# Adaptive layer norm, attention and mixture of experts on one core: layer-norm rows with a scalar-tensor-tensor, the input split on GpSimd, and two transposes ahead of the projection

## The chip, the cores and the metric

One core of one Trainium2 chip runs the whole program. The metric is the device time of one execution in microseconds (us); the number compared is the median of the runs. The engines are TensorE (PE, matmuls, with its weight loads PEld), VectorE (DVE), ScalarE (ACT), GpSimd (POOL) and SyncE (SP, which only issues DMAs here).

## The reference, cut to what matters

Eight batch items of 512 tokens with 128 channels go through an attention with 16 heads of 64, with normalised queries and keys, and then through a mixture of eight experts with a shared branch. The change touches the first part:

```python
h = _layernorm(x, axis=-1) * (1 + ca) + sa
x = x + ga * _L0_attn_ref(h, Wq, Wk, Wv, Wo, bo, q_scale, k_scale)
h = _layernorm(x, axis=-1) * (1 + cb) + sb
# in _L0_attn_ref, for each batch item b and head:
q = _l2norm(h @ Wq.T) * q_scale ; k = _l2norm(h @ Wk.T) * k_scale ; v = h @ Wv.T
attn = softmax(q @ k.T * DH ** -0.5) ; out = (attn @ v) @ Wo.T + bo
```

## The kernel before, in words

**Units and slots.** Work is cut into 64 units u = 8 b + hp: batch item b, head pair hp (two heads, 0 to 7). The attention loop has one slot for each unit, and a slot has four places, called `pair` in the code and counted from 0 to 3; place p handles the 128 query rows of tile p for both heads. Batch item 0 and the last one are written out, items 1 to 6 run in a hardware loop. Each engine has its own instruction stream in an order fixed by hand, and runs it in that order; semaphores are the only tie between engines. There is no scheduler.

**TensorE in one place of slot u.** `project` (L486 to L488) makes queries, keys and values of unit u+2 for one token tile, three matmuls in a split precision (a rounded high part and a low part); at place 0 one step of the residual stream follows (`between`: a part of the output projection L567 to L569, or a transpose of layer-norm rows L585, of y L577, or the router L593); at place 1 `inverse_rows` (L543) transposes the inverse row sums of unit u-1; at place 2 `transpose_q` (L495) transposes the normalised queries of unit u+1, at place 3 `transpose_k` (L502) its keys; then come `scores` (L516), `transpose_probs` (L532) and `weigh_values` (L556). All three transposes write one PSUM bank, XT_BANK, which is also the bank of `between`.

**The other engines in a slot.** ACT copies the projection out of PSUM (L676), copies the inverse rows (L707) and the high part of queries (L685) and keys (L690), and computes exponentials (L697). DVE takes the row maxima (L815), two at each place, the low parts of queries (L803) and keys (L810), the sum of squares of the next unit (L792) and at the slot's start the inverse of the row sums (L826). POOL starts its slot with `widen` (L993, waits for L826), then `normalise_qk`: twelve small Newton steps (L49 to L55) and two multiplications (L987), the first for queries and the second for keys, each with its own count of `qn_done`; then one square (L977), `split_o` (L999, L1001), and three more squares. `transpose_q` waits for the first L987.

**Layer norm.** In slots 0 and 3 of a batch item `norm_first` puts `ln_rows` (L200, four instructions of 128x128) at place 3 in front of the row maxima on DVE, and the TensorE transposes of those rows (L585) stand at place 0 of slots 1 and 4. These wait for `kl_done` as well, which L810 of place 3 sets after the row maxima. In slots 0 and 3 POOL also runs `inverse_std`, twelve more small steps, before its squares.

**The input split.** `split_h1` (L844, L846) turns the modulated input h1_out of the next batch item into a high part hT_h and a low part hT_l, one 128-token tile at a time. It runs on DVE, at places 1, 2 and 3 of slot 5 and place 0 of slot 6. Projections of the next item start in slot 6, place 0, and wait there for `hT_ready`. For item 0 the four tiles are split before the loop.

Of the kernel before, what the change touches and what calls it, by code (L numbers as in the profile page):

```python
# [5 lines left out]
P = 128  # L6
ALU = mybir.AluOpType
# [53 lines left out]
def adaln_attention_moe(nc, x, Wq, Wk, Wv, Wo, bo, q_scale, k_scale, proj_w, proj_b, expert_bias,  # L61
# [16 lines left out]
    with ExitStack() as whole:  # L78
# [62 lines left out]
        with ExitStack() as scope:  # L141
# [25 lines left out]
            def tile_of(b, t):  # L167

                return x1_all[:, bass.ds(b * NT + t, 1)].rearrange("p o c -> p (o c)")
# [26 lines left out]
            def ln_rows(dve, b, count):  # L196
                dve.wait_ge(ln_step, NEWTON_OPS * (count + 1))
                after(dve, hlnT_ready, count)
                for t in range(NT):
                    last = nc.vector.tensor_scalar(h_ln[:, t], tile_of(b, t), mean_var[:, t, 0:1], rstd[:, t:t + 1],  # L200
                                                   ALU.subtract, ALU.mult)
                last.then_inc(hln_done, 1)


# [258 lines left out]
            with nc.Block() as block:  # L463
# [13 lines left out]
                def _(pe):  # L477
# [144 lines left out]
                    def slot(b, hp, main=True):  # L622

                        u = HP * b + hp
                        earlier = units_before(b, hp)
                        side = (kl_done, u + 1 if main else u)
                        for pair in range(NT):
                            if main and with_next(b, hp, 2):
                                project(u + 2, hp + 2, b + (hp + 2) // HP, pair)
                            if main and pair == 0:  # L630
                                side = between(b, hp, u)
                            if pair == 1 and earlier >= 1:
                                inverse_rows(u - 1, side)
                                side = (r_copied, u)
                            if main and pair == 2 and with_next(b, hp, 1):
                                transpose_q(u + 1, hp + 1, side)
                            if main and pair == 3 and with_next(b, hp, 1):
                                transpose_k(u + 1, hp + 1)
                            if main:
                                scores(u, hp, pair)  # L640
                            if pair < 2 and earlier >= 1:
                                transpose_probs(u - 1, pair + 2)
                            if pair >= 2 and main:
                                transpose_probs(u, pair - 2)
                            if pair < 2 and earlier >= 2:
                                weigh_values(u - 2, hp - 2, pair + 2)
                            if pair >= 2 and earlier >= 1:
                                weigh_values(u - 1, hp - 1, pair - 2)
# [23 lines left out]
                def _(act):  # L672
# [59 lines left out]
                    def slot(b, hp, main=True):  # L732
                        u = HP * b + hp
                        earlier = units_before(b, hp)
                        for pair in range(NT):
                            if main and with_next(b, hp, 2):
                                copy_projection(u + 2, hp + 2, pair)
                            if pair == 0 and main:
                                if hp == Y_HP[0]:
                                    gate_y(b)  # L740
                                if hp == H1T_HP and not is_const(b, LAST):
                                    modulate1(b + 1)
                                if hp == H2T_HP and not is_const(b, 0):
                                    modulate2(b - 1)
                            if pair == 1 and earlier >= 1:
                                copy_inverse(u - 1, hp - 1)
                            if main and pair == 2 and with_next(b, hp, 1):
                                high_q(u + 1, hp + 1)
                            if main and pair == 3 and with_next(b, hp, 1):
                                high_k(u + 1, hp + 1)  # L750
                            if main:
                                exponentials(u, hp, 2 * pair)
                                exponentials(u, hp, 2 * pair + 1)
                            if pair == 1 and earlier >= 1:
                                copy_transposed(u - 1, hp - 1, 3)
                            if pair == 3 and main:
                                copy_transposed(u, hp, 1)
                            if main and pair == 1 and hp == H2T_HP and not is_const(b, 0):
                                keep_h2(b - 1)
# [27 lines left out]
                def _(dve):  # L787
# [49 lines left out]
                            last = nc.vector.tensor_copy(dst[:, k:k + 1], modT[:, v, bass.ts(b, 1)])  # L837
                        last.then_inc(done, 1)

                    def split_h1(b, t):  # L840
                        dve.wait_ge(h1_done, b + 1)
                        after(dve, pj_ready, NT * (HP * b - 1) + t + 1)
                        toks = slice(t * P, (t + 1) * P)
                        nc.vector.tensor_copy(hT_h[:, toks], h1_out[:, toks]).then_inc(h1h_done, 1)  # L844
                        dve.wait_ge(h1h_done, NT * b + t + 1)
                        nc.vector.tensor_tensor(hT_l[:, toks], h1_out[:, toks], hT_h[:, toks].bitcast(F32),  # L846
                                                ALU.subtract).then_inc(hT_ready, 1)

                    def add_y(b, k):
                        dve.wait_ge(y_ready, NT * b + k + 1)  # L850
                        if k == 1:
# [39 lines left out]
                    def norm_first(b, hp, pair):  # L891

                        rows = norm_of(b, hp)
                        if rows and pair == 1:
                            stats_there(dve, rows[1])
                        if rows and pair == 3:
                            ln_rows(dve, *rows)
                        if not is_const(b, LAST) and (hp, pair) in ((5, 1), (5, 2), (5, 3), (6, 0)):
                            split_h1(b + 1, (pair - 1) % NT)

                    def norm_last(b, hp, pair):

# [41 lines left out]
                            slot(b, hp)  # L944

                    take_mod(mod1, (CA, SA), 0, mod1_done, (h1_done, 0))
                    for t in range(NT):
                        split_h1(0, t)
                    sum_squares(0)
                    guess_norms(0)  # L950
                    low_q(0, 0)
# [19 lines left out]
                def _(pool):  # L971
# [17 lines left out]
                    def widen(u, hp):  # L989
# [4 lines left out]
                                                c1.unsqueeze(2).unsqueeze(3).to_broadcast([P, NT, 2, DH]),  # L994
                                                ALU.mult).then_inc(wide_done, 1)

                    def split_o(u, hp):
                        pool.wait_ge(o_done, u + 1)
                        nc.gpsimd.tensor_tensor(oT_h[:, hp % HP], oT[:], c1.to_broadcast([P, N]), ALU.mult).then_inc(oh_done, 1)  # L999
# [4 lines left out]
                    def slot(b, hp, main=True):  # L1004
# [14 lines left out]
                        if main and with_next(b, hp, 2):  # L1019
                            for t in range(1, NT):  # L1020
                                square_projection(u + 2, hp + 2, t)

                    def batch(b):
                        for hp in range(HP):
                            slot(b, hp)

                    normalise_qk(0, 0)
                    for t in range(NT):
                        square_projection(1, 1, t)
# [626 lines left out]
```

## Time and profile before

| | |
|---|---|
| median of 3 runs | 1407.26 us (1405.85 to 1416.08) |
| profiled execution, its own time | 1406.78 us |
| span of its instructions | 1405.0 us |
| mean granted TensorE clock | 0.959 of full speed |
| PE busy / DVE busy / ACT busy / POOL busy | 1262.1 / 1107.3 / 952.9 / 858.0 us |

The attention loop takes the stretch from about 43 to 1060 us, the routing and the experts the rest. In the timelines a row of several instructions (x4) gives the first start and the time from there to the last end. A bracket at a row's end gives the idle time of the engine in front of it and who ended it.

### The profile page before, as it was taken

What the parts mean: (1) busy time and instruction counts of PE and PEld (TensorE: products, weight loads), DVE (VectorE), ACT (ScalarE), POOL (GpSimd) and SP (SyncE); (2) the same over time, 40 slices, a digit from 0 to 9 for tenths busy, and PEclk for the clock granted to TensorE, in tenths of its full rate; (3) what the DMA queues carried; (4) which work ended last, traced back from release to release, by engine and by line L of the source; (5) the groups of instructions that cost most, each with busy time, mean ns of one, the idle gap of its engine ahead of it and who ended that gap; (6) DMA issues with size and microseconds to landing.
All of it is one profiled execution on the core that took longest, in us unless ns stands there. A gap on an engine that the chain in (4) does not pass through costs nothing. (4 is left out here: it accounts for less than half of the span.)

```text
span 1405.0 us, 31811 instructions
## 1 busy us (share of the span) xinstructions
PE 1262.1 (90%) x9674; PEld 828.6 (59%) x9674; DVE 1107.3 (79%) x1995; ACT 952.9 (68%) x2014; POOL 858.0 (61%) x1659
## 2 busy tenths in 40 slices
PE   4899999989999999999899999999994477899997
PEld 4555565656555565556566555666552355677775
DVE  3778878878878887788788788877873996788887
ACT  3677677767666776677677766777762565777776
POOL 2577666766666776666667667676754664444443
PEclk8899999999999999999999999999998699999999
DMA  5000000000000000000000000000002000535341
GB/s 131 2 2 1 2 1 2 2 4 2 1 4 2 2 2 4 2 2 2 4 1 2 3 2 2 2 1 2 2 1 75 1 0 9 131 86 104 89 89 38
DMA packets 53202, 28.60 MB, mean 20 GB/s; under 512 B 8720, under 2 KB 51224, under 8 KB 53016
## 3 DMA queue, kind: packets, MB, share of 16 engines
q1 hardware_dynamic: 51832, 25.99, 7.7%
q8 instruction: 84, 1.38, 0.4%
q14 instruction: 102, 0.84, 0.2%
q10 hardware_dynamic: 1184, 0.40, 0.1%
HBM read 24.16 MB, written 2.23 MB: 19 GB/s over the span
## 5 line engine op out<-in xcount | busy, mean ns | idle before, releaser
L697 ACT ACTIVATE probs<-bank,neg_max 128x512 f32<-128x512 f32 x512 | 347.5, 684 | 280.3 <-DVE neg_max L815 259.5
L815 DVE TENSOR_REDUCE neg_max<-bank 128x1 f32<-128x512 f32 x512 | 329.3, 685 | 165.4 <-PE bank L516 162.0
L556 PE MATMUL bank<-probsT,qkv 128*64 128x512 f32 x1024 | 280.7, 628 | 0.9 <-DVE oT L832 0.9
L516 PE MATMUL bank<-operands 64*128 64x512 f32 x1536 | 255.9, 439 | 0.9 <-DVE operands L810 0.5
L993 POOL TENSOR_TENSOR inv_wide<-inv_sum,consts 128x512 f32<-128x512 f32 x64 | 66.5, 1039 | 237.7 <-DVE inv_sum L826 237.7
L532 PEld LDWEIGHTS T<-ident,probs 64*128 64x128 f32 x4096 | 173.6, 142 | 40.3 <-issue 10.2
L532 PE MATMUL T<-ident,probs 64*128 64x64 f32 x4096 | 173.6, 226 | 1.5 <-issue 0.7
L486 PEld LDWEIGHTS bank<-operands,hT_h 128*128 128x128 f32 x254 | 48.2, 190 | 213.0 <-issue 209.4
L516 PEld LDWEIGHTS bank<-operands 64*128 64x128 f32 x1536 | 128.4, 190 | 63.5 <-issue 44.2
L1627 POOL TENSOR_TENSOR hid_l<-gated,hid_h 128x512 fp32r<-128x512 f32 x64 | 89.4, 1397 | 123.3 <-ACT hid_h L1544 123.3
L977 POOL TENSOR_TENSOR sq<-qkv 128x256 f32<-128x256 f32 x252 | 150.9, 615 | 11.9 <-ACT qkv L676 9.7
L821 DVE COPY probsT<-T 128x1024 f32<-128x1024 f32 x128 | 155.5, 1215 | 0.1
L1605 DVE TENSOR_TENSOR gated<-probsT,act_out 128x512 f32<-128x512 f32 x128 | 125.5, 990 | 36.5 <-ACT act_out L1558 24.2
L676 ACT ACTIVATE qkv<-bank 128x384 f32<-128x384 f32 x254 | 125.1, 493 | 21.5 <-PE bank L488 18.2
L987 POOL TENSOR_TENSOR qkv<-qkv,rn 128x512 f32<-128x512 f32 x128 | 131.5, 1048 | 5.0
L702 ACT ACTIVATE probsT<-T 128x1024 f32<-128x1024 f32 x128 | 130.8, 1022 | 0.1
L486 PE MATMUL bank<-operands,hT_h 128*128 128x384 f32 x254 | 113.1, 445 | 10.9 <-issue 9.4
L697 ACT ACTIVATION_READ_ACCUMULATOR probs<-bank,neg_max 128x1 f32 x512 | 100.8, 197 | 0.0
L1544 ACT ACTIVATE hid_h<-gated 128x512 fp32r<-128x512 f32 x128 | 80.3, 627 | 27.5 <-DVE gated L1605 26.9
L488 PE MATMUL bank<-operands,hT_l 128*128 128x384 f32 x254 | 86.9, 342 | 0.0
L487 PE MATMUL bank<-wqkv_l,hT_h 128*128 128x384 f32 x254 | 86.5, 341 | 0.0
L792 DVE TENSOR_REDUCE ss<-sq 128x16 f32<-128x1024 f32 x64 | 77.3, 1208 | 10.9 <-issue 7.1
(235 smaller groups left out, 2399.7 us busy)
## 6 DMA issues: line engine op xcount, KB each, us to landing
probsT<-gate_scratch SPq DMA_DIRECT2D x64, 256.0 KB, 4.9
out<-x_all SPq DMA_DIRECT2D x8, 256.0 KB, 2.3
probsT<-in_L_ffn_fc_w SPq DMA_DIRECT2D x1, 1024.0 KB, 9.4
raw<-in_L_attn_Wq SPq DMA_DIRECT2D x1, 512.0 KB, 4.4
raw<-in_L_attn_Wk SPq DMA_DIRECT2D x1, 512.0 KB, 7.3
raw<-in_L_attn_Wv SPq DMA_DIRECT2D x1, 512.0 KB, 8.6
raw_o<-in_L_attn_Wo SPq DMA_DIRECT2D x1, 512.0 KB, 8.7
probsT<-in_L_ffn_sh_w SPq DMA_DIRECT2D x2, 256.0 KB, 2.7
```

The source lines that it names most:

```text
L486: nc.tensor.matmul(o, hT_h[:, toks], wqkv_h[:, :, cols], start=True, stop=False)
L516: last = nc.tensor.matmul(s_bank(hp, 2 * pair + head)[:], own[rows, q, toks], own[rows, k], start=((q, k) == (QH, KH)), stop=(q == QL))
L532: last = nc.tensor.transpose(T2[:, half, at:at + DH], probs[rows, (2 * pair + head) % 4, j * P:(j + 1) * P], ident[rows, rows])
L556: last = nc.tensor.matmul(O_BANK[rows, :], qkv[:, hp % 4, j, cols], probsT[:, hp % 2, head, j], start=(j == 0), stop=(j == NT - 1), skip_g ...
L676: nc.scalar.activation(qkv[:, hp % 4, t], bank[:, 0:3 * P], ACT.Copy).then_inc(pj_copied, 1)
L697: nc.scalar.activation(probs[:, i % 4], s_bank(hp, i)[:], ACT.Exp, bias=neg_max[:, i:i + 1], accum_out=row_sum[:, hp % 2, i:i + 1]).then_i ...
L702: nc.scalar.activation(pair_tiles(hp, pair), t_pair, ACT.Copy).then_inc(t_act, 1)
L815: nc.vector.reduce_max(neg_max[:, i:i + 1], s_bank(hp, i)[:], AX.X, negate=True).then_inc(max_done, 1)
L821: nc.vector.tensor_copy(pair_tiles(hp, pair), t_pair).then_inc(t_dve, 1)
L977: nc.gpsimd.tensor_tensor(sq[:, t], qk, qk, ALU.mult).then_inc(sq_done, 1)
L987: nc.gpsimd.tensor_tensor(rows, rows, by, ALU.mult).then_inc(qn_done, 1)
L1605: nc.vector.tensor_tensor(gated[:, k % 4], gate_rows[:, k // 2], act_out[:, k % 4], ALU.mult).then_inc(gated_done, 1)
```

## The change

Three edits. First, `ln_rows` uses `scalar_tensor_tensor` in place of `tensor_scalar`: the mean is still a scalar per partition, but the inverse deviation is now a second tensor input in SBUF, broadcast along the row. Second, `split_h1` moves from DVE to POOL: the copy that rounded the high part becomes a multiplication by a column of ones, and all four tiles stand at the end of POOL's slot 5 (HP - 3), after the last square. For item 0 they stand in front of POOL's first `normalise_qk`. Third, in every slot `inverse_rows` at place 1 and `transpose_q` at place 2 stand in front of `project` on TensorE, and `copy_inverse` and `high_q` stand in front of `copy_projection` on ACT. The step `between` still follows the projection of place 0, and `transpose_k` that of place 3.

```diff
                 for t in range(NT):
-                    last = nc.vector.tensor_scalar(h_ln[:, t], tile_of(b, t), mean_var[:, t, 0:1], rstd[:, t:t + 1],
-                                                   ALU.subtract, ALU.mult)
+                    last = nc.vector.scalar_tensor_tensor(out=h_ln[:, t], in0=tile_of(b, t), scalar=mean_var[:, t, 0:1],
+                                                          in1=rstd[:, t:t + 1].to_broadcast([P, C]), op0=ALU.subtract,
+                                                          op1=ALU.mult)
...
                         for pair in range(NT):
-                            if main and with_next(b, hp, 2):
-                                project(u + 2, hp + 2, b + (hp + 2) // HP, pair)
-                            if main and pair == 0:
-                                side = between(b, hp, u)
                             if pair == 1 and earlier >= 1:
                                 inverse_rows(u - 1, side)
                                 side = (r_copied, u)
                             if main and pair == 2 and with_next(b, hp, 1):
                                 transpose_q(u + 1, hp + 1, side)
+                            if main and with_next(b, hp, 2):
+                                project(u + 2, hp + 2, b + (hp + 2) // HP, pair)
+                            if main and pair == 0:
+                                side = between(b, hp, u)
...
                         for pair in range(NT):
+                            if pair == 1 and earlier >= 1:
+                                copy_inverse(u - 1, hp - 1)
+                            if main and pair == 2 and with_next(b, hp, 1):
+                                high_q(u + 1, hp + 1)
                             if main and with_next(b, hp, 2):
                                 copy_projection(u + 2, hp + 2, pair)
...
-                        if not is_const(b, LAST) and (hp, pair) in ((5, 1), (5, 2), (5, 3), (6, 0)):
-                            split_h1(b + 1, (pair - 1) % NT)
...
+                    def split_h1(b, t):
+                        pool.wait_ge(h1_done, b + 1)
+                        after(pool, pj_ready, NT * (HP * b - 1) + t + 1)
+                        toks = slice(t * P, (t + 1) * P)
+                        nc.gpsimd.tensor_tensor(hT_h[:, toks], h1_out[:, toks], c1.to_broadcast([P, P]), ALU.mult).then_inc(h1h_done, 1)
+                        pool.wait_ge(h1h_done, NT * b + t + 1)
+                        nc.gpsimd.tensor_tensor(hT_l[:, toks], h1_out[:, toks], hT_h[:, toks].bitcast(F32),
+                                                ALU.subtract).then_inc(hT_ready, 1)
...
+                        if main and hp == HP - 3 and not is_const(b, LAST):
+                            for t in range(NT):
+                                split_h1(b + 1, t)
```

TensorE at place 2 of slot 2 of item 0, before. L486 to L488 are the projection, L495 the transposes of the queries, L516 the scores, L556 the weighted values of place 1, and a bracket names the semaphores waited for:

```order
L556 MATMUL bank<-probsT,qkv 64x512 x2
L486 MATMUL bank<-operands,hT_h 128x384 [waits pj_copied]
L487 MATMUL bank<-wqkv_l,hT_h 128x384
L488 MATMUL bank<-operands,hT_l 128x384
L495 MATMUL bank<-ident,qkv 128x128 [waits r_copied,qn_done]
L495 MATMUL bank<-ident,qkv 128x128 x3
L516 MATMUL bank<-operands 128x512 [waits p_done]
L516 MATMUL bank<-operands 128x512 x5
```

The same place after the change; each line number is one higher:

```order
L557 MATMUL bank<-probsT,qkv 64x512 x2
L496 MATMUL bank<-ident,qkv 128x128 [waits r_copied,qn_done]
L496 MATMUL bank<-ident,qkv 128x128 x3
L487 MATMUL bank<-operands,hT_h 128x384 [waits pj_copied]
L488 MATMUL bank<-wqkv_l,hT_h 128x384
L489 MATMUL bank<-operands,hT_l 128x384
L517 MATMUL bank<-operands 128x512 [waits p_done]
L517 MATMUL bank<-operands 128x512 x5
```

The transposes and their waits now stand directly behind the weighted values of the place before, and the projection stands between them and the scores. At place 1 the transposes of `inverse_rows` move in the same way.

POOL at the end of slot 5 and the start of slot 6 of item 0, before; L977 is the square, L993 `widen`:

```order
L999 TENSOR_TENSOR oT_h<-oT,consts 128x512 [waits o_done]
L1001 TENSOR_TENSOR oT_l<-oT,oT_h 128x512 [waits oh_done]
L977 TENSOR_TENSOR sq<-qkv 128x256 [waits pj_copied] x3
L993 TENSOR_TENSOR inv_wide<-inv_sum,consts 128x512 [waits r_ready,inv_done]
L49 TENSOR_TENSOR rn_t<-rn 128x16 [waits rn_guess]
L51 TENSOR_TENSOR rn_t<-rn_t,ss_half 128x16 [waits rn_step]
```

The same place after the change; L965 is the square, L989 and L991 are the split, L981 is `widen`, and the line of dots stands for three more pairs of L989 and L991:

```order
L998 TENSOR_TENSOR oT_l<-oT,oT_h 128x512 [waits oh_done]
L965 TENSOR_TENSOR sq<-qkv 128x256 [waits pj_copied] x3
L989 TENSOR_TENSOR hT_h<-h_out,consts 128x128 [waits pj_ready,h1_done]
L991 TENSOR_TENSOR hT_l<-h_out,hT_h 128x128 [waits h1h_done]
...
L981 TENSOR_TENSOR inv_wide<-inv_sum,consts 128x512 [waits r_ready,inv_done]
L49 TENSOR_TENSOR rn_t<-rn 128x16 [waits rn_guess]
```

The eight instructions of the split stand in front of `widen` of slot 6 and of the Newton steps behind it.

## Rows read from the trace of the kernel before

**Rows 1.** the page's first part: busy time of each engine

```profile
PE 1262.1 (90%) x9674; PEld 828.6 (59%) x9674; DVE 1107.3 (79%) x1995; ACT 952.9 (68%) x2014; POOL 858.0 (61%) x1659
```

**Rows 2.** who waited for whom: us in total, times, longest us

```profile
POOL inv_wide L993 <- DVE inv_sum L826: 237.7, 63, 5.7
...
PE bank L585 <- DVE operands L810: 33.2, 14, 2.7
...
PE bank L495 <- POOL qkv L987: 9.0, 10, 5.6
```

**Rows 3.** timeline of DVE, slot 3, place 3, item 4; start us, us taken, engine

```profile
609.67 3.40 DVE L200 TENSOR_SCALAR h_ln<-x_all,mean_var,rstd 128x128 f32 x4
```

**Rows 4.** timeline of POOL in the same stretch

```profile
610.02 1.04 POOL L999 TENSOR_TENSOR oT_h<-oT,consts 128x512 fp32r<-128x512 f32 x1
611.14 1.28 POOL L1001 TENSOR_TENSOR oT_l<-oT,oT_h 128x512 fp32r<-128x512 f32 x1
612.38 1.75 POOL L977 TENSOR_TENSOR sq<-qkv 128x256 f32<-128x256 f32 x3
```

**Rows 5.** timeline of TensorE, start of slot 4

```profile
615.02 1.08 PE L585 MATMUL bank<-ident,h_ln 128*128 128x128 f32 x4 [2.51 <-DVE operands L810]
```

**Rows 6.** busy time by stretch; the clock after the five engines

```profile
615.00:617.00 2.00, 1.98 (x8) 1.53 (x10) 1.54 (x5) 2.00 (x5) 0.31 (x1) 0.50 0.00 0
```

**Rows 7.** one line's instructions each: count, duration min/median/max in ns

```profile
L200 DVE TENSOR_SCALAR h_ln<-x_all,mean_var,rstd x64: 335/649/1443, 14.3 to 1083.0; 128x128 f32 x48, 128x128 f32<-128x128 f32 x16
...
L846 DVE TENSOR_TENSOR hT_l<-h_out,hT_h x32: 291/601/1143, 20.9 to 907.1; 128x128 fp32r<-128x128 f32 x32
```

**Rows 8.** timeline of DVE, slot 5 place 3 to slot 6 place 0

```profile
642.91 0.42 DVE L844 CAST hT_h<-h_out 128x128 fp32r<-128x128 f32 x1
643.36 0.60 DVE L846 TENSOR_TENSOR hT_l<-h_out,hT_h 128x128 fp32r<-128x128 f32 x1
...
645.09 0.68 DVE L810 TENSOR_TENSOR operands<-bank,operands 128x512 fp32r<-128x512 f32 x1
...
647.68 1.09 DVE L846 TENSOR_TENSOR hT_l<-h_out,hT_h 128x128 fp32r<-128x128 f32 x1
```

**Rows 9.** timeline of POOL in the same stretch

```profile
642.06 1.75 POOL L977 TENSOR_TENSOR sq<-qkv 128x256 f32<-128x256 f32 x3
647.58 1.04 POOL L993 TENSOR_TENSOR inv_wide<-inv_sum,consts 128x512 f32<-128x512 f32 x1 [3.77 <-DVE inv_sum L826]
```

**Rows 10.** timeline of TensorE, start of slot 6

```profile
644.97 0.44 PE L486 MATMUL bank<-operands,hT_h 128*128 128x384 f32 x1
...
645.91 0.47 PE L567 MATMUL bank<-oT_h,wo_h 128*128 128x512 f32 x1 [0.15 <-DVE operands L810]
```

**Rows 11.** timeline of TensorE, slot 3 place 2

```profile
604.30 0.44 PE L486 MATMUL bank<-operands,hT_h 128*128 128x384 f32 x1
...
605.11 0.66 PE L495 MATMUL bank<-ident,qkv 128*128 128x128 f32 x4
```

**Rows 12.** timeline of POOL, slot 3

```profile
604.00 2.06 POOL L987 TENSOR_TENSOR qkv<-qkv,rn 128x512 f32<-128x512 f32 x2
```

**Rows 13.** timeline of TensorE, slot 5 place 2

```profile
637.75 0.44 PE L486 MATMUL bank<-operands,hT_h 128*128 128x384 f32 x1
...
638.39 0.60 PE L495 MATMUL bank<-ident,qkv 128*128 128x128 f32 x4
```

**Rows 14.** timeline of POOL, slot 5

```profile
637.07 2.05 POOL L987 TENSOR_TENSOR qkv<-qkv,rn 128x512 f32<-128x512 f32 x2
```

**Rows 15.** timeline of TensorE, slot 6 place 2

```profile
653.42 0.44 PE L486 MATMUL bank<-operands,hT_h 128*128 128x384 f32 x1
```

**Rows 16.** timeline of POOL, slot 6

```profile
652.19 2.06 POOL L987 TENSOR_TENSOR qkv<-qkv,rn 128x512 f32<-128x512 f32 x2
```

**Rows 17.** timeline of TensorE, slot 2 of item 0, place 2

```profile
91.13 0.66 PE L495 MATMUL bank<-ident,qkv 128*128 128x128 f32 x4 [0.16 <-POOL qkv L987]
```

**Rows 18.** timeline of TensorE, first projection, before the loop

```profile
21.26 0.69 PE L486 MATMUL bank<-operands,hT_h 128*128 128x384 f32 x1 [1.46 <-DVE hT_l L846]
```

More of the change, by code:

```diff
@@ L744, in slot @@
                                     modulate2(b - 1)
[L745 to L748, printed above, removed]
                             if main and pair == 3 and with_next(b, hp, 1):
@@ L838, in take_mod @@
                         last.then_inc(done, 1)
[L840 to L847, printed above, removed]
                     def add_y(b, k):
@@ L946, in _ @@
                     take_mod(mod1, (CA, SA), 0, mod1_done, (h1_done, 0))
-                    for t in range(NT):
-                        split_h1(0, t)
                     sum_squares(0)
@@ L1025, in batch @@
                             slot(b, hp)
+                    for t in range(NT):
+                        split_h1(0, t)
                     normalise_qk(0, 0)
```

## The prediction

> **What bounds the kernel now.** I read the page's busy times first, then the list of who waited for whom, then single slots of the attention loop on every engine. TensorE is busy for 1262.1 of 1405.0 us [rows 1], and inside the loop it is the engine that sets the end: its pieces follow one another without a break but for a few places. POOL on the other hand waits 63 times, 237.7 us in all, at the start of its slot (3.8 us each) [rows 2]. So an instruction taken from DVE or given to POOL is worth nothing by itself. What counts is the handful of places where TensorE waits, and the places where it nearly waits.
>
> There are three kinds. First, the transposes of layer-norm rows at place 0 of slots 1 and 4 wait for DVE's L810: 14 times, 33.2 us [rows 2]; in item 4 the wait is 2.51 us, and the clock is at 0.50 of full speed (1.2 GHz) in the 2 us behind it [rows 5, 6]. DVE is late there because its four L200 take 3.40 us [rows 3] while POOL runs L999, L1001 and its squares [rows 4]. Second, the transposes of the queries wait for POOL's L987: 10 times, 9.0 us [rows 2]. Third, at the start of slot 6 the output projection L567 waits for L810 [rows 10]. The chains of the second kind matter most here, since the change takes away what stood in front of them.
>
> **The layer-norm rows: no gain expected.** The change would pay if the new instruction were not held up by POOL. In the rows L200 ends each time behind a POOL instruction: it starts at 609.67 and is through at 613.07, just behind the first of the three squares that begin at 612.38 [rows 3, 4]. One L200 took 335 ns at best and 649 in the median [rows 7], so the time is waiting and not work. Does an instruction with two tensor inputs in SBUF wait in the same way? The trace has one of the same size, L846: 291 ns at best, 601 in the median [rows 7]. In slot 6 it starts at 647.68, when POOL's L993 has run for 0.10 us, takes 1.09 us, and ends at 648.77, 0.15 behind the end of L993 at 648.62 [rows 8, 9]. So it waits for the whole of one POOL instruction, as L200 does. Four of them among POOL's queue of five should take what four L200 take: I add 0.06 us for each of 15 uses, because L846 ended 0.15 us behind POOL where L200 does so 0.09 us behind it: **+0.9 us**. The wait of L585 stays.
>
> The Trainium skill has the same in its page SBUF — State Buffer, section Who interferes with whom: a VectorE instruction with two SBUF inputs contends with a GpSimd instruction that reads SBUF, and a tensor_scalar in a two-port mode does too, for the whole instruction. By that rule, and the trace of L846 agrees, leaving tensor_scalar for a form with two SBUF inputs frees nothing. No row of before shows this form with a broadcast second input beside a busy POOL.
>
> **Inverse rows in front of the projection: nothing.** `widen` has ended in every slot of the loop before TensorE comes to place 1, so the transposes find their input even without the projection's 0.64 us ahead of them; in slot 6, where it runs latest against the DVE, it ends at 648.62 [rows 9]. `copy_inverse` on ACT changes places with a copy that nobody waits for there. If the cover is gone in a slot, the price is what is missing, under 0.1 us; I take 0 and put it into the range.
>
> **Queries in front of the projection: the main cost.** A projection takes 0.64 us until the next piece starts (637.75 to 638.39) [rows 13]. Before, TensorE ran it while POOL's first L987 finished; now the transposes ask 0.64 us earlier. They start 0.08 us after the end of that L987: in slot 3 it ends at 604.00 + 1.03 = 605.03, they start at 605.11 [rows 11, 12]. So a slot costs (end of the first L987 + 0.08 - start of place 2), not under 0 and not over 0.64, since then the projection is merely put behind.
> - Slot 3: 605.11 - 604.30 = 0.81 [rows 11, 12], capped: 0.64.
> - Slot 5: L987 ends at 637.07 + 1.03 = 638.10, so 638.18 - 637.75 = 0.43 [rows 13, 14].
> - Slot 6: 652.19 + 1.03 + 0.08 = 653.30 against 653.42: nothing, with 0.12 left [rows 15, 16]. Slots 2 and 7 look the same. Slots 0, 1 and 4 have more left, because the loop's edge or the wait of L585 lengthens their place 0.
>
> This pattern repeats in items 1 to 6: 6 x 1.07 = 6.4. In item 0, slots 0 to 4 have no work of an earlier item in `between`, and their transposes wait already (0.16 in four of the five) [rows 17]: 5 x 0.64 = 3.2. The last item pays in slots 1, 3, 4 and 5: 3 x 0.64 + 0.43 = 2.4. Sum **+12.0 us**. The delay of slot 3 isn't swallowed by the wait for L585 in slot 4: the scores of place 2 start 0.64 later, DVE's maxima, L200 and L810 with them.
>
> **The split.** DVE loses L844 and L846 at place 3 of slot 5, 0.42 + 0.60 us in front of the row maxima [rows 8]. L567 started 645.91 - 644.97 = 0.94 us after its projection [rows 10], 0.30 more than 0.64, for L810. That goes, with seven splits in the loop: **-2.1 us**. Elsewhere the split on DVE held up nobody.
>
> POOL gets eight instructions of 128 columns. From L999 (512 columns, 1.04 us) and a square (256 columns, 0.61, from 1.75 for three with overlap) [rows 4] 128 columns are some 0.40 us, from L1001 (1.28 at 512) some 0.45; with 0.08 for the wait between the two, a tile takes about 0.9 us and four take 3.6. The gap they go into runs from 643.81, the end of the squares, to 647.58, when `widen` starts [rows 9]: 3.77 us, so it is nearly filled. But DVE's small tensor_scalar instructions before the inverse sums can now meet them. They would be held up by up to 0.4 us each, with 1 us of relief ahead of them. Slot 6 has 0.12 us left [rows 15, 16]. I take 0.1 for each of seven, between 0 and 0.5: **+0.7 us**. The projection of slot 6 starts at 644.97 and needs the first tile, done at about 643.81 + 0.93 = 644.74 [rows 9, 10]: no wait, with 0.2 left, and the 0.43 of slot 5 on top of it. In front of the loop TensorE started its first projection at 21.26, right behind L846 [rows 18]; on POOL the first tile comes some 0.4 us later, and then TensorE is as slow as POOL is: **+0.4 us**.
>
> **Sum.** 0.9 + 12.0 - 2.1 + 0.7 + 0.4 = +11.9 us on the profiled execution's 1406.8, which is within 0.5 of the median: 1418.7 us, 0.8% slower. One per cent (14 us) is about what a measurement of this kernel tells from no change.
>
> **Rivals.**
> 1. *The new row instruction isn't held up by POOL.* Then four take at most 4 x 0.34 = 1.3 us in place of 3.4, the wait of L585 (2.4 on average) falls to about 0.4: 14 x 2.0 = 28 us. The slow clock behind the wait goes too: L585 took 1.08 us at the low level, and over a place I estimate 1.5 us, so 22 us. Slots 1 and 4 lose the slack that their wait gave them, 0.3 each, 4 us back. 1418.7 - 46 = 1373 us. It decides by whether the broadcast second input makes the instruction wait as L846 did. L846 speaks against it; nothing in before excludes it. Chance 0.13.
> 2. *POOL's chain becomes the bound in most slots.* If POOL's L987 comes later by more than the 0.12 us or little more that slots 2, 6 and 7 have, or TensorE gets to place 2 sooner, these pay up to 0.64 as well: 7 x 3 x 0.64 = 13.4, thus 1432 us. For it: margins this small, and splits that fill POOL's gap. Against it: they are steady, and only slot 6 has a split in front. Chance 0.15.
> 3. *The delays of the queries are absorbed*, because TensorE catches up at later waits (the loop's edge, L585). Then the sum is near 0: 1408 us. Chance 0.12.
>
> **How the numbers follow.** My forecast has 0.60. Its own range is 1412 to 1425: the cap on 18 or so slots may be 0.1 off each way, the split's terms go from 0 to 3.5. The range that should hold 8 in 10 goes from 1404 (rival 3 and some of its spread) to 1430 (forecast and most of rival 2), and leaves out rival 1 and the top. Slower by over 1% is over 1421.3: rival 2 and a fifth of the forecast, 0.27. Faster by over 1% is under 1393.2: rival 1 and a little, 0.14. The rest, 0.59, is within 1%.
>
> **What the profile after would show.** Right: L200's successor still takes 3.1 to 3.5 us for four; L585 still waits over 2 us and the clock still falls behind it; the transposes of the queries wait for L987 in slots 3 and 5 of each item and in slots 0 to 4 of item 0, 0.4 to 0.9 us each; POOL idles under 0.5 us before `widen` of slot 6; L567 there no longer waits. Wrong: four row instructions in 1.3 us and no wait of L585 (rival 1), or query waits in six slots of eight (rival 2).

## The result and the profile after

| | before | after |
|---|---|---|
| median, 6 runs each | 1408.1 us (1405.85 to 1416.08) | 1421.74 us (1418.19 to 1427.4) |
| profiled execution, span | 1405.0 us | 1425.7 us |
| mean granted clock of that execution | 0.959 | 0.950 |

The changed kernel takes 1.0093 times the time of before (95% interval 1.0061 to 1.0125), 13 us more. The forecast was 1418.7 us. The profiled execution is one of the slowest of the six. Their mean clocks and spans go together, from 0.959 with 1416.5 us to 0.950 with 1425.7 us, so up to some 9 us of the 20.7 between the two profiled executions go with the low clock of this one.

Line numbers up to L200 are as before; on TensorE and ScalarE they are one higher, the square is L965, the halves of split_o are L996 and L998, `widen` is L981, the multiplications of the norms L975, the split L989 and L991. Busy times on the page after; TensorE does the same work as in [rows 1], DVE 23.1 us less and POOL 27.5 us more:

```profile
PE 1263.8 (89%) x9674; PEld 824.5 (58%) x9674; DVE 1084.2 (76%) x1931; ACT 953.4 (67%) x2014; POOL 885.5 (62%) x1723
```

The list of who waited for whom in the kernel after (us in total, times, longest), to be read against [rows 2]:

```profile
POOL inv_wide L981 <- DVE inv_sum L827: 224.4, 63, 5.7
...
PE bank L586 <- DVE operands L811: 35.9, 14, 2.9
...
PE bank L496 <- POOL qkv L975: 23.3, 24, 5.0
```

The queries' transposes wait 24 times for 23.3 us where it was 10 times and 9.0. The layer-norm transposes still wait, a little longer than before (35.9 for 33.2). The timeline of DVE and of POOL at the place of [rows 3, 4], slot 3 of item 4, and the line's durations, as in [rows 7]:

```profile
618.66 3.69 DVE L200 SCALAR_TENSOR_TENSOR h_ln<-x_all,mean_var,rstd 128x128 f32<-128x128 f32 x4
```

```profile
618.57 1.04 POOL L996 TENSOR_TENSOR oT_h<-oT,consts 128x512 fp32r<-128x512 f32 x1
619.69 1.27 POOL L998 TENSOR_TENSOR oT_l<-oT,oT_h 128x512 fp32r<-128x512 f32 x1
620.92 1.90 POOL L965 TENSOR_TENSOR sq<-qkv 128x256 f32<-128x256 f32 x3
```

```profile
L200 DVE SCALAR_TENSOR_TENSOR h_ln<-x_all,mean_var,rstd x64: 339/697/1430, 14.2 to 1102.1; 128x128 f32<-128x128 f32 x64
```

The new form is held up like the old one. Four take 3.69 us where they took 3.40 and where I had said 3.1 to 3.5, and three squares take 1.90 where they took 1.75: now POOL is held up a little by DVE as well. Behind that, TensorE at the start of slot 4 and the granted clock of the stretch (the clock is the third figure from the end), to be read against [rows 5, 6]:

```profile
624.28 1.09 PE L586 MATMUL bank<-ident,h_ln 128*128 128x128 f32 x4 [2.80 <-DVE operands L811]
```

```profile
624.00:630.00 6.00, 5.71 (x32) 3.29 (x33) 4.23 (x9) 3.84 (x9) 3.26 (x12) 0.50 0.00 1
688.00:692.00 4.00, 3.19 (x8) 2.77 (x9) 1.80 (x5) 0.72 (x2) 1.41 (x3) 0.57 0.03 8
```

The wait is 2.80 us for 2.51, and now the clock is at the low level (0.50, 1.2 GHz) for the whole six us. The second row is the loop's edge of the same item: there TensorE idled 2.19 us (1.84 in the kernel before), and the clock fell too. The same two places in the kernel before have 0.79 over eight us, which is some 3.4 us at the low level, and no fall at the edge:

```profile
614.00:622.00 8.00, 6.98 (x61) 4.94 (x61) 5.36 (x11) 5.60 (x13) 4.50 (x15) 0.79 0.00 0
674.00:680.00 6.00, 4.16 (x35) 2.55 (x31) 3.71 (x9) 3.15 (x7) 0.50 (x2) 1.00 0.05 14
```

The two places where I had forecast the queries' wait, slot 3 and slot 5 of item 4:

```profile
613.54 0.66 PE L496 MATMUL bank<-ident,qkv 128*128 128x128 f32 x4 [0.79 <-POOL qkv L975]
```

```profile
648.69 0.66 PE L496 MATMUL bank<-ident,qkv 128*128 128x128 f32 x4 [0.40 <-POOL qkv L975]
```

The bracket gives 0.79 and 0.40 us; the forecast, from [rows 11 to 14], was 0.81 (capped to 0.64, since the projection follows) and 0.43. In item 0 five of these waits were forecast, for slots 0 to 4. The trace has six, in slots 0 to 5: 0.92 to 0.94 us in the last four of them, where before had 0.16 to 0.18. (The slot of [rows 17] is slot 3 of item 0, not slot 2; nothing hangs on it.)

In slots that wait for nothing the new order gives back a few hundredths of a us. From the last weighted values of place 1 (L556, then L557) to the first scores (L516, then L517) it was 2.16 us and is 2.13, in slot 4 of item 4, before and after:

```profile
621.99 1.08 PE L556 MATMUL bank<-probsT,qkv 128*64 128x512 f32 x4
...
624.15 0.97 PE L516 MATMUL bank<-operands 64*128 64x512 f32 x6
```

```profile
632.53 1.08 PE L557 MATMUL bank<-probsT,qkv 128*64 128x512 f32 x4
...
634.66 0.97 PE L517 MATMUL bank<-operands 64*128 64x512 f32 x6
```

In slot 6 of the same item the same stretch takes 2.31 us after. The queries' transposes come late there by too little for a bracket:

```profile
662.93 1.08 PE L557 MATMUL bank<-probsT,qkv 128*64 128x512 f32 x4
...
665.24 0.97 PE L517 MATMUL bank<-operands 64*128 64x512 f32 x6
```

In items 1 to 6 slot 6 takes 0.11 to 0.14 us longer than before, 0.7 us in sum. Last, POOL at the end of slot 5:

```profile
654.24 0.41 POOL L989 TENSOR_TENSOR hT_h<-h_out,consts 128x128 fp32r<-128x128 f32 x1
...
657.40 0.46 POOL L991 TENSOR_TENSOR hT_l<-h_out,hT_h 128x128 fp32r<-128x128 f32 x1
658.38 1.04 POOL L981 TENSOR_TENSOR inv_wide<-inv_sum,consts 128x512 f32<-128x512 f32 x1 [0.51 <-DVE inv_sum L827]
```

The split takes 654.24 to 657.86, 3.62 us, and POOL idles 0.51 us before `widen`, where it idled 3.77 [rows 9].

### The profile page after: what moved, and what is told of

The parts are those of the page before. It is cut to its first block and busy times, and to the rows that moved or that the text cites. A ratio compares the mean times of both kernels' runs of the same rounds, so it can differ in the third digit from the quotient of the medians.

```text
span 1425.7 us, 31829 instructions
## 1 busy us (share of the span) xinstructions
PE 1263.8 (89%) x9674; PEld 824.5 (58%) x9674; DVE 1084.2 (76%) x1931; ACT 953.4 (67%) x2014; POOL 885.5 (62%) x1723
## 5 line engine op out<-in xcount | busy, mean ns | idle before, releaser
L557 PE MATMUL bank<-probsT,qkv 128*64 128x512 f32 x1024 | 283.4, 634 | 0.9 <-DVE oT L833 0.9
L517 PE MATMUL bank<-operands 64*128 64x512 f32 x1536 | 255.2, 438 | 1.4 <-ACT probs L698 0.9
L981 POOL TENSOR_TENSOR inv_wide<-inv_sum,consts 128x512 f32<-128x512 f32 x64 | 66.5, 1039 | 224.4 <-DVE inv_sum L827 224.4
L517 PEld LDWEIGHTS bank<-operands 64*128 64x128 f32 x1536 | 128.3, 190 | 74.4 <-issue 50.4
L965 POOL TENSOR_TENSOR sq<-qkv 128x256 f32<-128x256 f32 x252 | 152.4, 621 | 7.8 <-ACT qkv L677 7.0
L975 POOL TENSOR_TENSOR qkv<-qkv,rn 128x512 f32<-128x512 f32 x128 | 131.6, 1049 | 5.0
L487 PE MATMUL bank<-operands,hT_h 128*128 128x384 f32 x254 | 111.4, 439 | 11.9 <-issue 10.0
L488 PE MATMUL bank<-wqkv_l,hT_h 128*128 128x384 f32 x254 | 87.0, 343 | 0.0
```

The costliest lines, as they stand in the source:

```text
L487: nc.tensor.matmul(o, hT_h[:, toks], wqkv_h[:, :, cols], start=True, stop=False)
L517: last = nc.tensor.matmul(s_bank(hp, 2 * pair + head)[:], own[rows, q, toks], own[rows, k], start=((q, k) == (QH, KH)), stop=(q == QL))
L557: last = nc.tensor.matmul(O_BANK[rows, :], qkv[:, hp % 4, j, cols], probsT[:, hp % 2, head, j], start=(j == 0), stop=(j == NT - 1), skip_g ...
L965: nc.gpsimd.tensor_tensor(sq[:, t], qk, qk, ALU.mult).then_inc(sq_done, 1)
L975: nc.gpsimd.tensor_tensor(rows, rows, by, ALU.mult).then_inc(qn_done, 1)
```

## The experiments

All ratios are against the kernel before, run beside it on the same chip, with 95% intervals.

**The three edits one by one.** Each is the kernel before with one edit of the change; the fourth moves only the queries.

```diff
 # e1_order: TensorE, and ScalarE in the same way
+inverse_rows at place 1 and transpose_q at place 2 in front of project
 # e2_rows: ln_rows
-nc.vector.tensor_scalar(h_ln[:, t], tile_of(b, t), mean_var[:, t, 0:1], rstd[:, t:t + 1], ...)
+nc.vector.scalar_tensor_tensor(out=h_ln[:, t], in0=tile_of(b, t), scalar=mean_var[:, t, 0:1],
+                               in1=rstd[:, t:t + 1].to_broadcast([P, C]), ...)
 # e3_split
-split_h1 on DVE, slots 5 and 6
+split_h1 on POOL, end of slot 5
 # e4_queries: of e1 only
+transpose_q (and high_q) in front; inverse_rows stays behind project
```

> The kernel before with the new order alone (inverse rows and queries in front of the projection on TensorE and ScalarE); rows and input split as before. My theory: nearly all of the loss is the queries' wait for POOL, +12.0 us, plus some more time at the low clock, since the waits of L585 become 0.2 us longer: 1.007 to 1.012 of before. Rival (the split and the rows carry half of it): 1.003 to 1.005.

> The kernel before with the scalar-tensor-tensor rows alone. My theory: held up by POOL as tensor_scalar is, 3.3 to 3.7 us for four in place of 3.1 to 3.4, so the wait of L585 grows by 0.2 to 0.3 us, 14 times, and the low clock behind it may last longer: 1.001 to 1.006 of before. Rival (the form frees DVE): under 0.975.

> The kernel before with the input split on GpSimd alone. My theory: -2.1 us for L567 in slot 6, +0.4 in front of the loop and about +0.7 in slot 6: 0.998 to 1.001 of before. Rival (the split delays POOL's chain and costs more than 0.3 us an item): 1.002 to 1.004.

> The kernel before with only the queries' transposes and their copy moved in front of the projection; inverse rows stay behind it. My theory: the same as the whole new order within 0.2%, since the inverse rows cost nothing. Rival (the inverse rows carry a part): less than two thirds of the loss of the whole order.

| | ratio | in us of 1409 | forecast |
|---|---|---|---|
| order alone | 1.0070 (1.0054 to 1.0086) | +9.9 | +12.0 |
| rows alone | 1.0046 (1.0032 to 1.0061) | +6.5 | +0.9 |
| split alone | 0.9977 (0.9961 to 0.9993) | -3.2 | -1.0 (-2.1 + 0.7 + 0.4); without the 0.7, which needs the new order, -1.7 |
| queries alone | 1.0064 (1.0048 to 1.0081) | +9.0 | as the order |

The three ratios multiply to 1.0093, which is the whole change. So no help or harm between the edits shows beyond the interval of the whole (1.0061 to 1.0125), and each term can be held against its forecast. The order and the rows came out in the range that I expected, the split 0.0003 below it. The order's loss is that of the queries: moving the inverse rows too makes no difference that the intervals show. In the order's run the queries wait as in the changed kernel, and L585 waits as before (list of waits), not 0.2 us longer each as I had expected:

```profile
PE bank L585 <- DVE operands L810: 32.6, 14, 2.7
...
PE bank L495 <- POOL qkv L987: 25.4, 28, 4.6
```

Five of these 28 waits stand in slots that the forecast called free: slot 1 of items 1 to 4 and slot 4 of item 6, 0.79 us or so each. In these five the clock had not fallen behind the wait of L585; in the other eight uses of slots 1 and 4 in items 1 to 7 it had, and the queries didn't wait. Two of them, slot 1 of item 4 and of item 5; first the granted clock, then TensorE:

```profile
567.00:575.00 8.00, 6.53 (x63) 3.98 (x63) 6.57 (x12) 6.71 (x18) 4.70 (x15) 1.00 0.00 1
698.00:706.00 8.00, 7.30 (x61) 4.74 (x63) 5.33 (x11) 5.41 (x13) 4.69 (x15) 0.79 0.01 3
```

```profile
567.69 0.63 PE L585 MATMUL bank<-ident,h_ln 128*128 128x128 f32 x4 [2.23 <-DVE operands L810]
...
575.03 0.65 PE L495 MATMUL bank<-ident,qkv 128*128 128x128 f32 x4 [0.81 <-POOL qkv L987]
...
698.70 0.63 PE L585 MATMUL bank<-ident,h_ln 128*128 128x128 f32 x4 [2.25 <-DVE operands L810]
...
706.70 0.66 PE L495 MATMUL bank<-ident,qkv 128*128 128x128 f32 x4
```

From L585 to the queries' transposes it is 7.34 us in the first case, of which 0.81 are the wait, and 8.00 in the second. So the slack of slots 1 and 4 came from the stretch at the low level, and not from the wait of L585 alone: where the clock stayed up, the queries' wait took back about half of what the clock had saved.

The rows alone make the wait of L586 2.4 us longer than in [rows 2], over 14 times; the four instructions take 3.27 to 3.81 us in the loop's uses where they took 3.07 to 3.59:

```profile
PE bank L586 <- DVE operands L811: 35.6, 14, 2.9
```

So 2.4 us of the 6.5 are longer waits. The rest goes with more time at the low clock. The granted clock is on record for each execution: its median is 0.951 over the 11 of the rows alone and 0.955 over the 22 of before beside them, while the split alone has 0.956 and the order alone 0.9545. 0.004 of the clock is some 11 us more at the low level; that costs at most half of it, 5.6 us (an estimate), and 4.1 us are left to explain. Where these 11 us lie isn't shown: the profiled execution of the rows alone (clock 0.953, before 0.959) has 19.0 us more, and of these 6.8 lie between 84 and 1056 us, the rest in front and behind. The split alone takes the wait of slot 6 away, and this timeline of TensorE is to be read against [rows 10]:

```profile
643.47 0.44 PE L486 MATMUL bank<-operands,hT_h 128*128 128x384 f32 x1
...
644.11 0.47 PE L567 MATMUL bank<-oT_h,wo_h 128*128 128x512 f32 x1
```

From projection to output projection it is 0.64 us now, where it was 0.94. In front of the loop the first projection of this run starts at 21.66 us, where [rows 18] have 21.26: 0.40 us later, as forecast.

```profile
21.66 0.69 PE L486 MATMUL bank<-operands,hT_h 128*128 128x384 f32 x1 [1.88 <-POOL hT_l L990]
```

**Does the wait for POOL make the order dear?** One of the three Newton steps of the query and key norms is left out, in the new order and in the old one. POOL's first multiplication then comes four small instructions earlier.

```diff
-    for k in range(3):
+    for k in range(2):        # for the query and key norms alone
```

> The kernel before with the new order alone, and with one of the three Newton steps of the query and key norms left out, so the norms are less exact. POOL's first multiplication then comes four small instructions, 1.2 us, earlier. My theory: the queries' waits (29.3 us by starts in the order's run, 12.1 in before) fall to about 5 in front of and at the head of the loop, and the loss of the order is gone: 0.994 to 1.001 of before. Rival (the order costs by what it does to TensorE's sequence, not by the wait for POOL): 1.004 or more.

> The control for the short chain: the kernel before, old order, with one of three Newton steps of the query and key norms left out (norms less exact). My theory: the chain being 1.2 us shorter takes the queries' waits away in both orders, so this kernel equals the new order with the short chain within 0.3%: 0.989 to 0.995 of before. Rival (the new order by itself is worth something once the chain is short): this is 0.996 or more.

New order with the short chain: 0.9916 (0.9897 to 0.9936). Old order with it: 0.9917 (0.9896 to 0.9938). Between the two the order costs nothing that the intervals show. The first came out faster than I had expected, and the control shows that the short chain is worth 0.8% in the old order too. Part of that are the old order's own queries' waits, 9.0 us before and 4.4 now; the rest of the 11.7 us (0.83%) isn't shown one by one, but in the profiled executions 6.8 of the 8.4 us between the two kernels are won before slot 1 of item 1. In both, the queries' transposes wait twice, in front of the loop or at its head (waits of the new order, then of the old one):

```profile
PE bank L495 <- POOL qkv L987: 4.4, 2, 4.1
```

```profile
PE bank L495 <- POOL qkv L987: 4.4, 2, 3.7
```

The other test of the same thing keeps all three Newton steps and gives the new order only to slots where the forecast's rule says that it is free. In short:

```diff
+use_new = not isinstance(b, int) and hp not in (3, 5)     # items 1 to 6, slots 0, 1, 2, 4, 6, 7
```

> The kernel before with the new order only in slots 0, 1, 2, 4, 6 and 7 of items 1 to 6, the slots where POOL's first multiplication ends before place 2 begins. My theory: no loss, 0.997 to 1.001 of before, while the whole order loses 0.7%. Rival (each moved transpose costs TensorE something): 1.003 or more.

0.9965 (0.9945 to 0.9984), 0.0005 below the range that I expected, and the queries' waits are no more than before:

```profile
PE bank L495 <- POOL qkv L996: 7.0, 10, 4.7
```

So 36 of the 64 slots can have the new order for nothing, or a small gain; the loss sits in the others. In this run's profile the clock fell behind all twelve waits of L585 in items 1 to 6, so slots 1 and 4 had their slack each time.

**Are the rows worth moving to an engine that doesn't meet POOL?** This prices my first rival without the form that was disputed: the rows are made on ScalarE.

```diff
+# POOL, behind inverse_std: neg_shift = -(mean * rstd), two instructions of 128x4
-# DVE, place 3 of slots 0 and 3: ln_rows, four instructions
+# ScalarE, same places, behind high_k:
+nc.scalar.activation(h_ln[:, t], tile_of(b, t), ACT.Identity, scale=rstd[:, t:t + 1], bias=neg_shift[:, t:t + 1])
```

> The kernel before (old order, split on DVE) with the layer-norm rows of slots 0 and 3 on ScalarE: POOL makes minus mean times inverse deviation in two small steps more, and four activations with scale and bias take the place of the four L200. No DVE instruction of the rows is left to be held up by POOL. My theory: the wait of L585 (about 46 us in 15 waits with L200 of the last item) falls to a few us, and the low clock behind it goes with it, 44 us at half speed, worth some 22 us: 0.955 to 0.970 of before. Rival (the rows aren't the cause, DVE is late anyway or ScalarE becomes the late one): over 0.985.

> The same with the input split on GpSimd too. My theory: the split is worth 0.2% as it was alone: 0.002 below the kernel with the rows on ScalarE. Rival (POOL, now with two more steps, becomes late in slot 6): no better or worse than it.

> The changed kernel in full (new order, split on GpSimd) but with the rows on ScalarE. My theory: the new order costs what it did, and more, since slots 1 and 4 lose the slack that their wait gave the queries: 0.008 to 0.014 above the kernel with rows and split alone. Rival (the order costs only because of the stalls around it): within 0.003 of it.

| | ratio |
|---|---|
| rows on ScalarE | 0.9926 (0.9907 to 0.9944) |
| and split on POOL | 0.9890 (0.9873 to 0.9907) |
| and the new order | 0.9976 (0.9963 to 0.9988) |

The gain was 0.7% and not the 3 to 4.5% that I expected. Of the 14 waits of the layer-norm transposes for the keys' low part (L810) one of 0.9 us is left, in item 0, and the median of the mean clock rose from 0.955 to 0.966. But other waits took their place. These are rows of the list of waits, and of the timeline at the start of slot 4 of item 4, of the kernel with the rows on ScalarE (L815 is the sum of squares, L849 the inverse sums, L998 the square, L1014 `widen`, L562 the inverse rows on TensorE):

```profile
DVE ss L815 <- POOL sq L998: 33.2, 13, 3.3
...
PE bank L562 <- POOL inv_wide L1014: 18.3, 14, 1.9
PE bank L514 <- POOL qkv L1008: 16.9, 20, 4.7
```

```profile
607.87 1.75 POOL L998 TENSOR_TENSOR sq<-qkv 128x256 f32<-128x256 f32 x3
...
610.11 1.22 DVE L815 TENSOR_REDUCE ss<-sq 128x16 f32<-128x1024 f32 x1 [3.26 <-POOL sq L998]
...
611.74 0.20 DVE L849 RECIPROCAL inv_sum<-row_sum 128x8 f32<-128x8 f32 x1
...
612.02 1.04 POOL L1014 TENSOR_TENSOR inv_wide<-inv_sum,consts 128x512 f32<-128x512 f32 x1 [2.40 <-DVE inv_sum L849]
...
613.12 0.66 PE L562 MATMUL bank<-ident,inv_wide 128*128 128x128 f32 x4 [1.85 <-POOL inv_wide L1014]
```

POOL's squares end at 609.62, late because this slot has the twelve steps of the layer norm too. DVE has been idle for 3.26 us when it can start the sum of squares; the inverse sums stand behind that in DVE's order, `widen` behind them, and TensorE waits 1.85 us for the inverse rows at place 1. So two chains ended close to each other, the second at most 2 us behind, and L200's had hidden POOL's. About half of these 2 us is this experiment's own doing: POOL makes neg_shift in front of its squares, and from the start of the norms' multiplications to the end of the last square it takes 11.01 us here (598.61 to 609.62) and 10.13 in the kernel before (604.00 to 614.13):

```profile
598.61 2.06 POOL L1008 TENSOR_TENSOR qkv<-qkv,rn 128x512 f32<-128x512 f32 x2
...
604.21 0.20 POOL L201 TENSOR_TENSOR neg_shift<-mean_var,rstd 128x4 f32<-128x4 f32 x1
```

It is 0.88 us more in slot 3 of each item, and 0.6 us or more in slot 0. So the 0.7% prices the rows off DVE together with this load on POOL, and not the first alone.

The new order costs 0.9% again on top of this (0.9976 against 0.9890). The inverse rows wait longer in it too, 24.6 us for 17.5, where they hardly waited in either order while L585 waited in front of them; no run here moves them alone. The list of waits of the kernel with rows and split, and of that with the new order too (in both L995 is the norms' multiplication and L1001 `widen`):

```profile
PE bank L514 <- POOL qkv L995: 18.2, 22, 4.8
...
PE bank L562 <- POOL inv_wide L1001: 17.5, 14, 1.6
```

```profile
PE bank L514 <- POOL qkv L995: 35.3, 36, 5.6
...
PE bank L562 <- POOL inv_wide L1001: 24.6, 15, 2.3
```

**Both chains shortened.** The last pair leaves out one Newton step of three in all norms (they are less exact), with rows on ScalarE and the split on POOL, in the old and in the new order.

```diff
-    for k in range(3):
+    for k in range(2):        # all norms; NEWTON_OPS = 8
```

> Rows on ScalarE, split on GpSimd, old order, and one Newton step of three left out of both the query and key norms and the layer norms (both less exact). What held up the kernel with rows on ScalarE is POOL's chain in slots 0 and 3: its squares come late, the sum of squares on DVE waits for them, and the inverse sums stand behind it. My theory: with 2.4 us less on POOL there, the waits of the inverse rows (20 us) and of the queries (22 us) fall to some 8 together: 0.965 to 0.978 of before. Rival (another engine takes over, DVE or ScalarE): over 0.982.

> The same with the new order. My theory: where the chain is short enough the order costs nothing: within 0.003 of the kernel with the old order. Rival (it still costs 0.9%).

Old order: 0.9564 (0.9541 to 0.9588), 1352.03 us. New order: 0.9573 (0.9551 to 0.9594), 1352.3 us. That is more than I expected, and the fastest kernel of this study. Rows on ScalarE with the split gave 1.1%, the short chain of the query and key norms alone 0.8%, and the last pair 4.4%, more than twice the sum. Two readings are left. Either each edit alone only uncovers the other's chain, or the layer norm's step does it, which only this pair leaves out: it stands in POOL's chain of slots 0 and 3 and is 1.1 us of it (four instructions of 0.28 us each, from start to start). The kernel with rows on ScalarE and only the query and key norms shortened wasn't run. The page's busy times and the remaining wait of the queries in the old order:

```profile
PE 1245.8 (92%) x9674; PEld 822.8 (61%) x9674; DVE 1030.2 (76%) x1875; ACT 972.0 (72%) x2070; POOL 823.9 (61%) x1432
```

```profile
PE bank L514 <- POOL qkv L995: 4.1, 2, 3.4
```

TensorE is busy for 1245.8 of 1351.9 us, and of the waits of the layer-norm transposes and the inverse rows the loop has one left, 0.9 us in item 0. The order is free again, as far as the intervals show.

## Why the prediction was right, point by point

**Direction, cause and size of the whole** were right: +13 us against +11.9, and the loss is that of the queries' transposes waiting for POOL. But three terms were off and happened to cancel: the rows were 5.6 us too low, the queries 2.1 and the split 2.2 too high. That the sum is so close is luck. Only the error of the rows is clear of the intervals; the forecast of the queries lies inside, that of the split at the edge.

**The queries, +12.0: measured +9.9** (7.6 to 12.1), by the slots that the rule named: 0.79 and 0.40 us waited in slots 3 and 5, and a loss that disappears with a shorter chain or in the slots with slack. The forecast lies inside the interval. Still the trace shows what it left out, on both sides. It left out the waits in slot 5 of item 0 and in slots 1 and 4 where the clock stayed up. And it left out the gain where nothing waits: in the run of the order alone each group of transposes that is moved, queries or inverse rows, brings the scores forward by 0.03 to 0.04 us, in some 90 places, 3 us or so in all (an estimate).

**Inverse rows, 0: right**, as far as the queries alone cost the same as both. With the rows on ScalarE, where no wait of L585 stands in front of them and POOL's chain is longer, they waited.

**The rows, +0.9: measured +6.5.** That the form is held up by POOL was right; the step that failed is the size, "I add 0.06 us for each of 15 uses". It is 0.2 to 0.3 us for four instructions, because I counted how far the last of them ends behind POOL (0.15 us for 0.09) and took POOL's own instructions to stay as they are. They get longer: the four L200 wait for four of them in turn, and three squares took 1.90 us in place of 1.75. With the rows on ScalarE they took 1.75 again. And I priced a longer wait at its own length, though [rows 6] showed the low clock behind it. In the rows' own run the longer waits are 2.4 us and the larger part goes with the lower mean clock, as far as the clocks on record show.

That the longer wait itself keeps the clock low for longer is not shown. In the changed kernel the low stretch lasted six us behind four of the six waits of 2.79 to 2.81 us in slot 4, and 3.4 us behind the other two. But in the run of the queries alone it lasted as long behind two waits of 2.51 and 2.52 us, which are as long as those of before:

```profile
620.84 1.08 PE L585 MATMUL bank<-ident,h_ln 128*128 128x128 f32 x4 [2.51 <-DVE operands L810]
```

```profile
620.00:628.00 8.00, 7.16 (x39) 4.54 (x41) 4.78 (x10) 4.97 (x13) 4.55 (x14) 0.57 0.00 0
```

The Trainium skill, page SBUF — State Buffer, section Who interferes with whom, names a VectorE instruction with two SBUF inputs as one that contends with GpSimd reads. The traces of the changed kernel and of the rows alone agree, for a second input that is broadcast along the row: 339 ns at best, 697 in the median.

**The split, -1.0 in sum: measured -3.2** (-5.5 to -1.0). The relief in slot 6 is the 0.30 us an item forecast, and the 0.40 us in front of the loop came as well. The +0.7 for slot 6 could not show in the split alone, since there the projection still covers the queries; in the changed kernel it came, with 0.7 us over six items. What is left is -1.7 forecast against -3.2, inside the interval. The tiles took 0.90 us each as estimated, POOL was ready 0.51 us before `widen` could start, and of the small DVE instructions one met a hold-up, 0.40 us for 0.17 (timeline of DVE in the kernel after, L798 is the first of them):

```profile
657.50 0.40 DVE L798 TENSOR_SCALAR ss<-ss 128x16 f32<-128x16 f32 x1
```

**Rival 1** fell: the form is held up. Its price of 46 us is doubtful too: the rows on ScalarE gave about 10 us, with up to 12 us more on POOL in the same places (14 uses of up to 0.88, an estimate). The price took the wait that ended last for the only one. **Rival 2** didn't happen in the change, but for the 0.1 us in slot 6. It is what happened with the rows on ScalarE, where POOL's chain was the next bound. **Rival 3** is out: the order alone costs 0.5 to 0.9%.

## What to carry to other kernels

When a wait is to be removed, list for the same place every other input that is due there and when it came: here a 2.5 us wait hid a second chain that was 1 to 2 us behind (1.85 us measured, of which 0.88 came with the experiment); taking work off one of them gave about 1% each time, and the kernel that shortened both gave 4.4%. When an instruction with a wait is moved ahead of work that doesn't need it, the cost is what its input is late by, capped by the length of the work it passes; that can be read slot by slot from the trace of before, and it says in which slots the move is free. Ask too what the slack of a slot rests on: in slots 1 and 4 it rested on a stretch at the low clock, and where the clock stayed up the slack was gone.

## What the runs showed that I had not expected

- The four L200 on DVE and the queue of POOL instructions went in turns: each L200 ended just behind one POOL instruction, and the one that met L998 took 1.43 us. With two tensor inputs DVE held POOL up as well (three squares 1.90 us for 1.75), with tensor_scalar it did not: they took 1.75 us beside it as well as without it.
- The spread between executions of one kernel goes with the granted clock: six executions of the changed kernel have 0.950, 0.950, 0.954, 0.955, 0.957 and 0.959, with spans of 1425.7, 1425.6, 1420.8, 1419.1, 1418.1 and 1416.5 us. The same wait is not always followed by the same clock: in the run of the order alone the clock fell behind eight of the thirteen waits of L585 in items 1 to 7 (2.2 to 2.7 us each), and not behind the other five.
